# Two residual blocks of group norm and convolution (3x3, 5x5): trimmed matmul columns, a shorter setup, a new order around step 4, and TensorE jumping through three pages of its code

## What is computed

```python
def _gn(v, G=16, eps=1e-05): ...        # group norm without weights, 2 channels a group
x = x + _L0_conv_ref(_gn(x), w3, threshold)   # 3x3, padding 1; see the mask
x = x + _L1_conv_ref(_gn(x), w5, bias)        # 5x5, padding 2, written with an FFT
# the mask of the 3x3 weights, for each input channel and tap:
score = sum(abs(weight), axis=0) / 32
mask  = (score - max(threshold, 0) > 0)
mask0 = (score > 0);  mask = mask0 if mean(mask) <= 0.01 else mask
```

## Time and profile before

| | |
|---|---|
| median of 3 runs | 815.8 us (815.01 to 816.04) |
| the profiled execution | 814.5 us, span 812.7 us, granted clock of TensorE 0.985 |
| PE busy | 751.7 us, 92% of the span, 32292 matmuls |
| DVE busy | 615.3 us, 76% |
| ACT busy | 332.3 us, 41% |
| POOL busy | 264.6 us, 33% |
| chain that ended last | PE 85%, DMA 5%, SP's queue 4%, DVE 3% |
| DMA | 150.49 MB, mean 185 GB/s, busy 8 or 9 tenths in most slices up to 600 us |
| queue "instruction" (q8) | 10 packets, 0.16 MB |

### The profile page before, as it was taken

How to read it: one execution, slowest core, us unless ns; L and a number is a source line. 1 busy time by engine, 2 the same in 40 slices (tenths; PEclk the granted TensorE clock), 3 DMA queues, 4 the chain that set the end, 5 groups by cost and what they waited for, 6 DMA issues and landing times.

```text
span 812.7 us, 67805 instructions
## 1 busy us (share of the span) xinstructions
PE 751.7 (92%) x32292; PEld 503.0 (62%) x32292; DVE 615.3 (76%) x971; ACT 332.3 (41%) x287; POOL 264.6 (33%) x161
## 2 busy tenths in 40 slices
PE   0776689999999999999999999999999999999996
PEld 0442347777666666666666666666666666666564
DVE  6888488787878789797878789697878796663541
ACT  0341316353443436353444436353443436362420
POOL 1050033222334443222334343322334343322360
PEclk9998899999999999999999999999999999999999
DMA  8999489898997979898997979898997956573424
GB/s 186 195 199 224 112 176 230 211 218 201 221 217 178 219 174 222 196 223 194 217 223 164 237 168 227 191 224 196 217 221 186 216 116 163 137 165 86 104 52 103
DMA packets 234176, 150.49 MB, mean 185 GB/s; under 512 B 18656, under 2 KB 227616, under 8 KB 230048
## 3 DMA queue, kind: packets, MB, share of 16 engines
q1 hardware_dynamic: 227168, 144.00, 80.8%
q10 hardware_dynamic: 6272, 4.90, 2.3%
q0 software_dynamic: 704, 1.25, 0.6%
HBM read 75.60 MB, written 33.59 MB: 134 GB/s over the span
## 4 chain that ended last, share of the span: by engine, by line
PE 85%; DMA 5%; SPq 4%; DVE 3%; issue 1%; DVEq 0%; ACT 0%; ACTq 0%
PE psum L873 65%; PE psum L891 20%; DMA x_bands<-x_dram 3%; SPq L271 1%; DVE bn_in L626 1%; SPq L263 1%; SPq L252 1%; DMA mv_scratch<-mv 1%; DMA every_mv<-mv_scratch 1%; DVE x_lo L730 1%; ACT conv_out L477 0%; DVE x_bands L702 0%; SPq L278 0%; DVE mid L750 0%; DVEq L753 0%
## 5 line engine op out<-in xcount | busy, mean ns | idle before, releaser
L376 POOL TENSOR_TENSOR mid<-mid,conv_out 128x512 f32<-128x512 f32 x118 | 241.2, 2075 | 481.5 <-ACT conv_out L477 481.5
L873 PE MATMUL psum<-x_hi,s_hi 32*64 32x512 f16 x6656 | 199.6, 383 | 16.4 <-ACTq L517 8.3
L873 PE MATMUL psum<-x_lo,s_hi 32*64 32x512 f16 x6656 | 197.5, 380 | 6.3 <-DVE x_lo L730 5.3
L873 PE MATMUL psum<-x_hi,s_lo 32*64 32x512 f16 x6656 | 196.5, 377 | 1.4 <-issue 1.4
L873 PEld LDWEIGHTS psum<-x_hi,s_hi 32*64 32x64 f16 x6656 | 107.3, 105 | 98.5 <-ACTq L517 10.2
L873 PEld LDWEIGHTS psum<-x_hi,s_lo 32*64 32x64 f16 x6656 | 127.0, 104 | 58.9 <-issue 2.8
L873 PEld LDWEIGHTS psum<-x_lo,s_hi 32*64 32x64 f16 x6656 | 102.6, 104 | 87.2 <-issue 9.8
L750 DVE SCALAR_TENSOR_TENSOR mid<-psum,unscale,x_own 128x1024 f32<-128x1024 f32 x64 | 79.2, 1278 | 97.8 <-PE psum L891 97.8
L400 ACT ACTIVATE x_hi<-x_bands 128x2304 f16<-128x2304 f32 x31 | 65.7, 2118 | 117.9 <-PE psum L891 117.8
L477 ACT ACTIVATE conv_out<-psum,bias,unscale 128x512 f32<-128x512 f32 x118 | 82.2, 776 | 70.7 <-PE psum L873 62.6
L738 DVE TENSOR_TENSOR x_lo<-mid_bands,x_hi 128x2560 f16<-128x2560 f32 x32 | 92.3, 2885 | 4.1 <-PE psum L873 4.0
(11 more groups left out here) (92 smaller groups left out, 348.6 us busy)
## 6 DMA issues: line engine op xcount, KB each, us to landing
x_own<-x_dram SPq DMA_DIRECT2D x128, 256.0 KB, 5.0
mid_bands<-mid SPq DMA_DIRECT2D x372, 80.0 KB, 2.7
out_dram<-mid SPq DMA_DIRECT2D x112, 256.0 KB, 5.4
x_bands<-x_dram SPq DMA_DIRECT2D x96, 288.0 KB, 5.9
x_bands<-x_dram SPq DMA_DIRECT2D x32, 272.0 KB, 6.8
mid_bands<-mid SPq DMA_DIRECT2D x124, 64.0 KB, 2.6
every_mv<-mv_scratch ACTq DMA_DIRECT2D x16, 256.0 KB, 3.8
out_dram<-mid SPq DMA_DIRECT2D x28, 128.0 KB, 2.4
```

Of the source, the lines that this page charges most:

```text
L376: nc.gpsimd.tensor_tensor(m, m, conv_out[:, b, :], ALU.add).then_inc(out_added, 1)
L873: ins = nc.tensor.matmul(psum[2 * C * J:2 * C * (J + 1), bank + i, :].rearrange("p (a w) -> p a w", a=A), w[quad(i), at:at + 2, :].rearran ...
```

## The change

- `pairs` and `singles` leave out the columns that would only meet the zeros beside the picture: taps one column off stream 4 x 127, taps two off 4 x 126. The centre tap, which is full, goes first, because it sets the bank anew.
- Setup: the threshold is loaded first on ACT's queue, with a semaphore of its own; the bound of the 3x3 weights is taken before the mask; both sums over the partitions are done in one; nine products are one; `unscale` is made last. Half 2 of `x` is loaded ahead of w5. `largest(w5)` moves behind `stats_in(3)` and `set_apart("x", 1)`.
- POOL scales w5 after the first eight DMAs of half 1, and makes its low part after twelve.
- DVE, end of the lead: `stats_in(6)` and `stats_in(7)` move ahead of the wait for the gathered statistics of image 2, `low3(4)` behind the aggregates.
- TensorE's loop is cut into `whole_step`, `conv5`, `conv5_more` and `conv5_last`, with a branch at the end of each, and between them lie three stubs of two instructions. TensorE's first branch goes to the first stub (`fetch_second`), which branches to the next one, and the last to `lead_start`.

The declarations of the larger `across` and `turned` and of two semaphores (`thr_loaded`, `code_touched`) are left out here.

```diff
--- before.py
+++ after.py
@@ -105,8 +105,8 @@
         ones = sbuf("ones", [P, P])
-        across = sbuf("across", [P, C])
-        turned = sbuf("turned", [P, C])
+        across = sbuf("across", [P, 2, C])
+        turned = sbuf("turned", [P, 2, C])
         total = sbuf("total", [P, 2])
@@ -287,9 +289,9 @@
             load_bands(1)
+            load_bands(2)
             for q in range(Q):
                 sp.dma_start(w5[quad(q), :, :], w5_dram.rearrange("i a b o -> i (a b) o")).then_inc(w_loaded, 16)
-            load_bands(2)
             load_bands(3)
@@ -364,10 +366,12 @@
                     pool.dma_start(to, rows).then_inc(mid1_moved, 16)
-            pool.wait_ge(w5_bounded, 1)
-            nc.gpsimd.tensor_scalar(w5[:, :, :], w5[:, :, :], wfac[:, 1:2], None, ALU.mult).then_inc(w5_scaled, 1)
-            pool.wait_ge(w5_hi_made, 1)
-            nc.gpsimd.tensor_tensor(s5_lo[:, :, :], w5[:, :, :], s5_hi[:, :, :], ALU.subtract).then_inc(w5_split, 1)
+                if i == 1:
+                    pool.wait_ge(w5_bounded, 1)
+                    nc.gpsimd.tensor_scalar(w5[:, :, :], w5[:, :, :], wfac[:, 1:2], None, ALU.mult).then_inc(w5_scaled, 1)
+                elif i == 2:
+                    pool.wait_ge(w5_hi_made, 1)
+                    nc.gpsimd.tensor_tensor(s5_lo[:, :, :], w5[:, :, :], s5_hi[:, :, :], ALU.subtract).then_inc(w5_split, 1)
 
@@ -491,9 +495,9 @@
 
+            act.dma_start(thr[:, :], thr_dram.rearrange("(a o) -> a o", a=1).to_broadcast([P, 1])).then_inc(thr_loaded, 16)
             for q in range(Q // 2, Q):
                 act.dma_start(w3[quad(q), :, :], w3_dram.rearrange("i a b o -> i (a b) o")).then_inc(w3_loaded, 16)
-            act.dma_start(thr[:, :], thr_dram.rearrange("(a o) -> a o", a=1).to_broadcast([P, 1])).then_inc(w3_loaded, 16)
             act.dma_start(mix_in[:, :], mix_dram).then_inc(mix_loaded, 16)
@@ -571,9 +575,11 @@
 
-                own_step(nc.vector.tensor_scalar(across[:, :], ones[:, 0:C], src, None, ALU.mult))
-                own_step(nc.vector.transpose(turned[:, :], across[:, :]))
-                own_step(nc.vector.tensor_reduce(to, turned[:, :], AX.X, ALU.add))
+                n = src.shape[1]
+                own_step(nc.vector.tensor_copy(across[:, 0:n, :], src.unsqueeze(2).to_broadcast([P, n, C])))
+                own_step(nc.vector.transpose(turned[:, 0:n, :].rearrange("p n c -> p (n c)"),
+                                             across[:, 0:n, :].rearrange("p n c -> p (n c)")))
+                own_step(nc.vector.tensor_reduce(to, turned[:, 0:n, :], AX.X, ALU.add))
 
@@ -583,13 +589,16 @@
                 at = slice(n, n + 1)
-                over_partitions(total[:, at], bound[:, at])
                 own_step(nc.vector.tensor_scalar(power[:, at], total[:, at], 2.0 ** -100, None, ALU.max))
...
                 own_step(nc.vector.tensor_scalar(wfac[:, at], wfac[:, at], WTOP, None, ALU.mult))
-                own_step(nc.vector.tensor_scalar(unscale[:, at], power[:, at], 1.0 / (WTOP * PIX), None, ALU.mult))
+
+            def undo_power(n):
+
+                at = slice(n, n + 1)
+                nc.vector.tensor_scalar(unscale[:, at], power[:, at], 1.0 / (WTOP * PIX), None, ALU.mult)
 
@@ -599,24 +608,24 @@
 
-                dve.wait_ge(w3_loaded, 16 * (Q + 1))
+                dve.wait_ge(w3_loaded, 16 * Q)
                 own_step(nc.vector.tensor_reduce(score[:, :], w3[:, :, :], AX.X, ALU.add,
                                                  apply_absolute_value=True))
+                largest(w3, 0)
+                dve.wait_ge(thr_loaded, 16)
                 own_step(nc.vector.tensor_scalar(small[:, 0:1], thr[:, :], 0.0, None, ALU.max))
-                own_step(nc.vector.tensor_scalar(mask[:, :], score[:, :], 1.0 / C, small[:, 0:1], ALU.mult, ALU.subtract))
-                own_step(nc.vector.tensor_scalar(mask[:, :], mask[:, :], 0.0, None, ALU.is_gt))
+                own_step(nc.vector.tensor_scalar(mask[:, :], score[:, :], 1.0 / C, small[:, 0:1], ALU.mult, ALU.is_gt))
                 own_step(nc.vector.tensor_scalar(mask0[:, :], score[:, :], 1.0 / C, 0.0, ALU.mult, ALU.is_gt))
-                own_step(nc.vector.tensor_reduce(small[:, 1:2], mask[:, :], AX.X, ALU.add))
-                over_partitions(small[:, 3:4], small[:, 1:2])
-                own_step(nc.vector.tensor_scalar(small[:, 2:3], small[:, 3:4], 1.0 / (C * T3), 0.01,
+                own_step(nc.vector.tensor_reduce(bound[:, 1:2], mask[:, :], AX.X, ALU.add))
+                over_partitions(total[:, 0:2], bound[:, 0:2])
+                own_step(nc.vector.tensor_scalar(small[:, 2:3], total[:, 1:2], 1.0 / (C * T3), 0.01,
                                                  ALU.mult, ALU.is_le))
                 own_step(nc.vector.scalar_tensor_tensor(mask[:, :], mask0[:, :], small[:, 2:3], mask[:, :], ALU.mult, ALU.max))
-                for t in range(T3):
-                    ins = nc.vector.tensor_scalar(w3n[:, t, :], w3[:, t, :], mask[:, t:t + 1], None, ALU.mult)
-                own_step(ins)
-                largest(w3n, 0)
+                own_step(nc.vector.tensor_tensor(w3n[:, :, :], w3[:, :, :], mask[:, :].unsqueeze(2).to_broadcast([P, T3, C]),
+                                                 ALU.mult))
                 power_of_two(0)
                 split_w3()
+                undo_power(0)
 
@@ -779,8 +788,6 @@
             set_apart("x", 0)
-            dve.wait_ge(w_loaded, 16 * Q)
-            largest(w5, 1)
             dve.drain().then_inc(bank3_go, 1)
@@ -790,6 +797,8 @@
             set_apart("x", 1)
+            dve.wait_ge(w_loaded, 16 * Q)
+            largest(w5, 1)
             take_conv3(0)
@@ -797,7 +806,9 @@
             low3(2)
+            over_partitions(total[:, 1:2], bound[:, 1:2])
             power_of_two(1)
+            undo_power(1)
             nc.vector.drain().then_inc(w5_bounded, 1)
@@ -811,17 +822,17 @@
             stats_out(2)
+            stats_in(2 * LAG, range(BANKS))
+            stats_in(2 * LAG + 1, range(BANKS))
             dve.wait_ge(mv_in, 16)
...
             stats_out(LAG)
-            low3(LAG + 1)
-            stats_in(2 * LAG, range(BANKS))
-            stats_in(2 * LAG + 1, range(BANKS))
             aggregate("mid", LAG // 2)
             aggregate("x", LAG, mv_ready)
+            low3(LAG + 1)
 
@@ -861,37 +872,41 @@
         def _(pe):
-            def pairs(w, src, k, bank, start=False, every=None):
-
-                for dx in range(k):
+            def columns(k, part=slice(None)):
+
+                for dx in sorted(range(k), key=lambda d: abs(d - k // 2))[part]:
                     x0 = 2 - k // 2 + dx
+                    yield dx, x0, max(0, 2 - x0), min(W, W + 2 - x0)
+
+            def pairs(w, src, k, bank, start=False, every=None, part=slice(None)):
+
+                for dx, x0, c0, c1 in columns(k, part):
                     for dy in range(1, k):
...
                                 ins = nc.tensor.matmul(
-                                    psum[2 * C * J:2 * C * (J + 1), bank + i, :].rearrange("p (a w) -> p a w", a=A),
+                                    psum[2 * C * J:2 * C * (J + 1), bank + i, :].rearrange("p (a w) -> p a w", a=A)[:, :, c0:c1],
                                     w[quad(i), at:at + 2, :].rearrange("p t o -> p (t o)"),
-                                    src[quad(i), top:top + A * (A - 1) + 1:A, x0:x0 + W],
-                                    start=start and dx == 0 and dy == 1, stop=True, skip_group_check=True,
+                                    src[quad(i), top:top + A * (A - 1) + 1:A, x0 + c0:x0 + c1],
+                                    start=start and dx == k // 2 and dy == 1, stop=True, skip_group_check=True,
                                     tile_position=(i * C, 2 * C * J))
...
 
-            def singles(w, src, k, bank, start=False):
-
-                for dx in range(k):
-                    x0 = 2 - k // 2 + dx
+            def singles(w, src, k, bank):
+
+                for dx, x0, c0, c1 in columns(k):
                     for i in range(Q):
...
                             ins = nc.tensor.matmul(
-                                psum[quad(j), bank + i, :].rearrange("p (a w) -> p a w", a=A), w[quad(i), at, :],
-                                src[quad(i), j + dy:j + dy + A * (A - 1) + 1:A, x0:x0 + W],
-                                start=start and dx == 0, stop=True, skip_group_check=True, tile_position=(i * C, j * C))
+                                psum[quad(j), bank + i, :].rearrange("p (a w) -> p a w", a=A)[:, :, c0:c1], w[quad(i), at, :],
+                                src[quad(i), j + dy:j + dy + A * (A - 1) + 1:A, x0 + c0:x0 + c1],
+                                start=False, stop=True, skip_group_check=True, tile_position=(i * C, j * C))
                 return ins
@@ -912,12 +927,6 @@
 
-            def pairs5_high():
-
-                pe.wait_ge(x5_hi_go, 1)
```

(30 more changed lines are left out.)

2 lines of the change are left out of this document (added).

## The result

| | before | after |
|---|---|---|
| median (17 runs each) | 815.6 us (813.7 to 818.65) | 817.5 us (816.06 to 819.38) |
| ratio after / before | | 1.0022 (95% interval 1.0012 to 1.0033) |
| profiled execution, span | 812.7 us | 815.4 us |
| packets of code (queue "instruction") | 10 | 11 |

The change makes the kernel 0.2% slower; 812.1 us had been forecast. The time stays inside the range, the direction was wrong.

What follows compares the result with a forecast made beforehand. TensorE alone bounds from 113 us, in 22.80 us steps; the lead's waits come before. -4.3 - 5.5 + 0.2 + 5.9 = -3.7 takes the profiled 814.5 to 810.8; the median, 1.3 higher, is 812.1 us, range 805.5 to 820.0.

Steps and rivals of the forecast that it cites:

- part 6: TensorE's stubs at the start: page fetches delay the first mix to 27.1 us and take_conv3(0) to 41.7, +5.9 us.
- part 2: Fewer columns in the side taps of conv 3 and conv 5: 0.18 us less per step, -5.5 us in all.
- too late: Rival on the stubs: page behind the last stub fetched ahead of lead_start, or 9 us each; 819.0 us; chance 0.20.
- if the array's rhythm is not set by columns the gain is 0: Rival on trimmed taps: step stays 22.80, 817.6 us; chance 0.07, shared with the jumps showing.
- Part 1: DVE's statistics moved into idle time at the lead's end: conv 5 of step 4 starts at 108.6, not 112.95, -4.3 us.
- the 1.5 us: Lower clock after idle time in the first 160 matmuls from 112.95: possible gain counted as nothing, left to the range.
- Parts 3 and 5: Three more jumps per TensorE step: hidden, 0, taken as +0.2 us; POOL's reordered w5 scaling and half 1 pieces: 0.
- Part 4: Shorter setup, earlier threshold, reordered loads: -0.3 us (0 to -0.5), lost behind the late mix.
- FIFO: Reading of the skill's rule on TensorE's code store: touched pages gone by 70 us, gaps stay, sum unchanged.

Runs made afterwards that it cites:

- e1: The changed kernel with TensorE's first branch going straight to lead_start, no stub entered: 808.0 us, ratio 0.989 to the kernel before.
- e7: The changed kernel with the first stub returning to the lead, so one stub is entered: 809.0 us, ratio 0.9924 to the kernel before.
- e9: The changed kernel with SP waiting for the third stub before loading halves 1, 2 and w5: 812.8 us, one run.
- e4: As e1, but all taps stream all 512 columns, cut loop and centre tap first kept: 807.5 us, ratio 0.9892 to the kernel before.
- e3: The kernel before with only DVE's new order at the end of the lead: 810.15 us, ratio 0.9918.
- e10: The changed kernel with its stubs, but DVE's old order at the end of the lead: 824.5 us, ratio 1.0113 to the kernel before.
- e6: As e4, but the loop in one piece, without the three jumps and the stub blocks: 806.2 us, ratio 0.9875 to the kernel before.
- e8: As e6, but column taps in their old order, left to right: 808.9 us, ratio 0.9922 to the kernel before.

## Why the prediction was wrong, point by point

Two terms of the sum failed, part 6 by 4.1 us and part 2 by 4.2. Either one alone would have left the forecast at no change; only both together turn it.

**Part 6, the stubs: the price of a page.** The path was right: the late mix goes to `take_conv3(0)` (14.94 us from one to the other, 14.6 forecast), nothing makes up for it, the loaded pages have no gap, a later one has, and the gaps are off the path or nearly so (0 forecast; 0.1 us by e1, 0.4 in e7). The size was not: +9.96 for +5.9. The first two pages were there at 11.2 (13 forecast). The next two, at 7.05 each, "the mean of 5.1 and 9.0", took 9.0 and 10.5 (11.2 to 20.2 to 30.7). The mean was the fault: the text says itself that the queues stay full until 38 us, so the higher price was the one to use. Its 9.0, used twice, gives 31 against the measured 30.7, but by luck in part: the 13 it starts from is 1.8 too high, and the last branch took 1.5 more than 9.0. That extra comes with the second packet of the last branch; the prediction has a page behind the last stub only in the rival "too late", at a whole page's price. With 31 the sum would have been 816.0, no change. Also misread was the price with idle queues: from 90.29 to 98.06 TensorE is busy 6.6 of 7.7 us (granted clock 0.63), so 3.9 us a page is mostly running time; a fetch with no other traffic took 2.81 (e9).

**Part 2, columns: mis-sized.** -5.5 forecast; the loop as a whole gave 22.76 for 22.80, some -1.3 from conv 5 of step 4 on. The trimming has 0 to 0.03 us a step of it, the cut of the loop the rest. The prediction knew that a group takes 10 ns more than its columns; from that I should have asked what sets the rhythm. In the steady steps twenty groups of conv 5 take 4.36 us with all columns (e4) and 4.36 to 4.39 with 507 on the mean (e1, after). So "if the array's rhythm is not set by columns the gain is 0" was the case, near enough; it had 0.07. What sets it instead was not tried.

**Part 1, step 4: right**, -4.2 for -4.3, with its mechanism: `group_stats` starts at 104.66, behind the wait for half 7 (102.27), x3_lo comes last (0.38 of waiting) and ACT's evictions end before it. **The clock behind it was left out of the sum, and should not have been**: the 1.5 us was given up since "the new idle time is about as long". It is (2.58 us before 112.53), but it now ends ahead of conv 3 of half 4 instead of ahead of conv 5. The granted clock is 0.72 from 112.5 to 118.7, a stretch that waits for DVE's x3_lo anyhow, and 1.00 from 118.7 on. Gain 1.73, shown again by e3 (4.40 for 6.07, where TensorE waits only 0.51 us for x3_lo) and by e10.

**Parts 3 and 5: right.** The three branches per step, by line:

```profile
L989 PEldq COMPARE_BRANCH  x29: 177/177/199, 76.1 to 732.5; - x29
L997 PEldq COMPARE_BRANCH  x32: 169/177/179, 81.7 to 794.7; - x32
L1003 PEldq COMPARE_BRANCH  x32: 169/171/171, 84.3 to 797.3; - x32
```

They take 169 to 199 ns each, not the 51 that the prediction gives for a plain branch; they last some 0.52 us together and lie beside the array's work; the step is not longer for them, but 0.03 us shorter (e4 and e6). POOL's order moved nothing that a run shows.

**Part 4, setup: right in the sum** (lost behind the late mix), small by itself. Where TensorE is in time, the mix starts at 19.8 to 21.0 (e1, e4 to e8) against 21.25, 0.3 to 1.5 us earlier where 0 to 0.5 was given: it follows the landing of half 1, as foreseen, but that came at 16.1 to 17.6 and not at 17.7.

**The sum again**, in terms of the span: +9.96 for +5.9 is +4.1; columns -1.3 for -5.5 is +4.2; the clock -1.7; the order and the jumps -0.1. That is 6.5 above -3.7, +2.8; measured +2.7.

**The rule of the Trainium skill** (Runtime: NRT & Kernel Launch, Instruction fetch mechanics) says that a taken branch out of a two-page window forces a fetch that execution waits for. The four branches of 4.0 to 10.2 us agree, as stalls. The window of two pages does not: pages touched at 5 to 20 us run without a gap at 77 to 87 us, and a loop of eight pages runs its 27 steady steps with one code packet of TensorE's queue after 130 us, of 11 in all. The prediction's step from "FIFO" to touched pages that are gone by 70 us does not follow from that section, and the trace is against it.

## What to carry to other kernels

To load code early is a fetch like any other: it waited longer the more loads had been issued ahead of it (2.8 us with none under way, 8.75 with three halves of x and w5), and whoever makes an engine touch its pages while the first inputs stream in holds that engine through them. Before touching pages, look whether the gaps they would remove end last; here 9.3 us of gaps did not. When a side of a sum is priced by rows, take the row whose state (queues full, clock) is that of the place, not the mean of two states. When a step is read from a chain, take many steps: one step of e6 shows 22.76, the mean of 25 is 22.79. And where an idle time moves, ask which instructions then run at the lower clock.
